# A graph layer on one core: tables on 96 partitions, weights split stepwise, loads between portions of the clear, and a reordered second stage

## The chip, the core and the metric

The kernel runs on one NeuronCore of a Trainium2 chip. The core has five engines with queues of their own: TensorE (PE, with its weight loads PEld), VectorE (DVE), ScalarE (ACT), GpSimd (POOL) and SyncE (SP), which here only issues DMAs. They meet through semaphores. The metric is device time in microseconds (us), the median of several runs.

## The reference

50,000 nodes with 256 features and 50,000 edges, sorted by `dst`. In the call the layer's `idx_i` is `src` and its `idx_j` is `dst`. Everything is float32.

```python
def ssp(x): return jax.nn.softplus(x) - LOG2
h = x @ W_in2f
Wij = (ssp(rbf @ Wf1 + bf1) @ Wf2 + bf2) * dist_cut     # rbf: edge_attr_64
x_ij = h[idx_j] * Wij
m = jax.ops.segment_sum(x_ij, idx_i, num_segments=n_atoms)
m = ssp(m @ Wo1 + bo1) @ Wo2 + bo2
return _layernorm(x + (x + m))
```

## The kernel before

**Groups.** Edges are worked on in G = 98 groups of 512 (the last has 336), as R = 4 rows r of 128. Since the edge sum and the product with Wo1 can change places, the first stage computes for each group: gather `x[dst]` (`xg`, a ring of 8), transpose it, h = x W_in; in parallel the filter from `attr`; the message; its product with Wo1; a product with `same` that adds up edges of equal `src` within the group; and a scatter with addition into the DRAM tensor `acc`. `acc` must first be filled with bo1 - log 2 (the "clear"). The second stage goes over the nodes in 98 groups: fetch `acc`, transpose, softplus, product with Wo2 plus bo2, residual 2x + m, normalisation, store.

**Precision.** Each product is three: every operand is split into a high part (`_h`, type float32r) and a low part (`_l`). ScalarE makes the high parts, VectorE the low ones.

**Order.** Each engine has its order written out: `run((stage, lag), ...)` issues in step s, for each entry, the stage for group s - lag. There is no scheduler.

**Start (before).** VectorE zeroes three tables (L649 to L651); SP then loads dst, bo1, src and the edge weights as tables of 97 rows of 2 KB plus one short row, then all weights and biases (L255 to L261), then issues the clear: 195 DMAs of 256 KB and two more (L265, L267). TensorE turns the tables (L377); VectorE copies `dst_t`, after which GpSimd may gather; VectorE splits all the weights (L683 to L697), and its last operation releases `const_made`, for which TensorE and ScalarE wait ahead of step 0.

**First stage.** GpSimd issues gathers for AHEAD = 21 groups, each waiting until TensorE has turned the x eight groups back (`xt_ps`); only then the scatter of group 0, which also waits for the whole clear; then scatters and the remaining gathers alternate. `sums` is a ring of 11 between `keep_y` and the scatter. ScalarE issues the loads of `attr` and `src` (L525, L530) within its step, just ahead of `keep_y(0)` (L607). The second stage's first eight `xg` loads (L280) wait for the last x transposes.

**Second stage.** The lines of a step s are, by engine:

```python
pe:   run((turn2(0), 0), (out2(0), 2), (turn2(1), 0), (out2(1), 2))
act:  run((expo2, 0), (ssp2_high, 1), (loga2, 0), (deviation, 3))
dve:  run((cap_2, 0), (ssp2_low, 1), (softplus_2, 0), (residual, 2))
pool: run((norm, 0))
```

`turn2` (L494) transposes one half of the features; `out2(q)` (L506, L509) computes two rows r: for each a product of `ones_r` with `bo2_hl`, both on 2 partitions (high and low part of bo2), and six products on 128. `expo2` is L621, `cap_2` (L784, clamp at 2^57 and add 0.5) comes between it and the logarithm `loga2` (L626), `softplus_2` (L790) takes the maximum with the input, `ssp2_high` is L631, `ssp2_low` L674, `residual` L808 (with sums) and L813 (negative mean), `deviation` four squares with sums (L640). On GpSimd `norm` computes the variance plus eps (L357), its power -1/2 (L359) and the four normalised rows (L363). `res` has three buffers (DEPTH), `normed` four; the residual of group g waits for the normalisation of group g - 3.

Of the kernel before, what the change touches and what calls it, by code (L numbers as in the profile page):

```python
# [50 lines left out]
AHEAD = 21  # L51
LOG2 = 0.6931471805599453
EXP_MAX = 2.0 ** 57
# [24 lines left out]
def build(nc, t, out):  # L78
# [7 lines left out]
    TAIL = E - (G - 1) * ROWS  # L86

# [3 lines left out]
    def run(*stages, start=0):  # L91

        for s in range(start, G + max(lag for _, lag in stages)):
            for stage, lag in stages:
                if 0 <= s - lag < G:
                    stage(group(s - lag))
# [3 lines left out]
    with ExitStack() as ctx:  # L103
# [12 lines left out]
        ones = sb("ones", [2, P])  # L116
        ones_r = sb("ones_r", [2, P], F32R)
# [18 lines left out]
        dst_t = sb("dst_t", [P, R, G], I32)  # L136
        spare_i = sb("spare_i", [P, 1], I32)
# [35 lines left out]
        squares = attr[:, 0:2].rearrange("p u r k a -> p (u r k a)").rearrange("p (r d) -> p r d", r=R)  # L173
# [16 lines left out]
        const_made = sem("const_made")  # L190
# [51 lines left out]
        def _(sp):  # L242

            def load_rows(dest, ap, done):
                sp.dma_start(dest[0:G - 1, :], ap[0:(G - 1) * ROWS].rearrange("(g e) -> g e", e=ROWS)).then_inc(done, 16)
                sp.dma_start(dest[G - 1:G, 0:TAIL], ap[(G - 1) * ROWS:E].rearrange("(g e) -> g e", e=TAIL)).then_inc(done, 16)

            sp.wait_ge(rows_zero, 1)
            load_rows(dst_i, t["dst"], dst_in)
            sp.dma_start(bo1[:], t["L0_gnn_bo1"].partition_broadcast(P)).then_inc(bo1_in, 16)  # L250
            load_rows(src_i, t["src"], rows_in)
            load_rows(wgt_f, t["edge_weight1"].rearrange("e a -> (e a)"), rows_in)

            for k in range(2):
                sp.dma_start(wf1[k * A:(k + 1) * A, :], t["L0_gnn_Wf1"]).then_inc(const_in, 16)  # L255
            for w, name in ((w_in, "L0_gnn_W_in2f"), (wf2, "L0_gnn_Wf2"), (wo1, "L0_gnn_Wo1"), (wo2, "L0_gnn_Wo2")):
                sp.dma_start(w[:], t[name].rearrange("(h p) n -> p h n", p=P)).then_inc(const_in, 16)
            for b, name in ((bf1, "L0_gnn_bf1"), (bf2, "L0_gnn_bf2")):
                for h in range(H):
                    sp.dma_start(b[:, h:h + 1], t[name][h * P:(h + 1) * P].rearrange("(p a) -> p a", a=1)).then_inc(const_in, 16)  # L260
            sp.dma_start(bo2[:], t["L0_gnn_bo2"].partition_broadcast(2)).then_inc(const_in, 16)  # L261

            sp.wait_ge(fill_made, 1)
            for c in range(CLEARS):
                sp.dma_start(acc[c * CLEAR * P:(c + 1) * CLEAR * P, :].rearrange("(p k) d -> p (k d)", k=CLEAR), fill[:, 0:CLEAR].rearrange("p k d -> p (k d)")).then_inc(cleared, 16)  # L265
            for a, b in ((CLEARS * CLEAR * P, N), (N, N + R * P)):
                sp.dma_start(acc[a:b, :].rearrange("(p k) d -> p (k d)", k=4), fill[0:(b - a) // 4].rearrange("p k d -> p (k d)")).then_inc(cleared, 16)  # L267

# [18 lines left out]
            for n in range(XRING):  # L287
                fetch_x(group(n))
# [13 lines left out]
        def _(pool):  # L302
# [4 lines left out]
            pool.memset(ones[:], 1.0).then_inc(made, 1)  # L307
            pool.iota(spare_i[:], [[0, 1]], base=N, channel_multiplier=1).then_inc(made, 1)
# [62 lines left out]
        def _(pe):  # L371

            pe.wait_ge(made, 6)
            for k, (rows, arrived, count, done) in enumerate(((dst_f, dst_cast, 1, dst_ps), (src_f, rows_cast, 1, tab_ps), (wgt_f, rows_in, 16 * 4, tab_ps))):
                pe.wait_ge(arrived, count)
                for r in range(R):
                    last = pe.transpose(bank[k][:, r * G:(r + 1) * G], rows[0:G, r::R], ident[0:G, 0:G])  # L377
                last.then_inc(done, 1)

            pe.wait_ge(two_made, 1)  # L380
            for m in range(H):
                for k in range(H):
# [452 lines left out]
```

## Time and profile before

| | us |
|---|---|
| median of 3 runs | 2085.95 |
| lowest, highest | 2079.63, 2088.7 |
| profiled execution | 2090.3 |
| its span, first to last instruction | 2088.5 |
| busy TensorE / VectorE / ScalarE / GpSimd | 1886.3 / 1637.4 / 1550.2 / 1535.3 |
| mean granted clock of TensorE, 1 is full speed | 0.98 |

Busy time alone tells little here: a matmul's end is modelled, so TensorE at 90% is not TensorE at its peak, and on GpSimd the issuing of gathers and scatters counts as work. In the timeline a row is: start, duration, engine, line, operation, output <- inputs, and in brackets how long the engine was idle before it and what ended that. Rows with "x4" are several instructions in one.

### The profile page before, as it was taken

The page shows a single profiled execution, that of the slowest core. Times are in us where ns is not written, and L with a number is a line of the kernel's source. Part 1 is how long each engine was busy: PE and PEld are TensorE (multiplying, and loading weights), DVE is VectorE, ACT ScalarE, POOL GpSimd, SP SyncE. Part 2 cuts the span into 40 slices and gives each one's busy share as a digit, 9 for nine tenths or more (in the row PEclk, how much of TensorE's full clock was granted, in tenths as well). Part 3 has the DMA queues.
Part 4 walks back from the last instruction along what each step waited for, and adds up shares of the span by engine and source line. Part 5 has one row for each costly group of instructions (what it writes and reads, how often), then busy time and mean ns, then how long its engine had stood idle before and what let it go on. Part 6 is the DMA issues. An engine that isn't in the chain of part 4 may idle for free. (4 is left out here: it accounts for less than half of the span.)

```text
span 2088.5 us, 37484 instructions
## 1 busy us (share of the span) xinstructions
PE 1886.3 (90%) x11780; PEld 1606.7 (77%) x11780; DVE 1637.4 (78%) x3663; ACT 1550.2 (74%) x3137; POOL 1535.3 (74%) x1384
## 2 busy tenths in 40 slices
PE   1899999999999999999999898895999999999997
PEld 1788888888888888888887787784777777777775
DVE  2788888888888888888888877783677777777774
ACT  0777888778787787887787776672777777777775
POOL 5422788888888888888888888763677777777776
PEclk9999999999999999999999999996999999999997
DMA  6999566666666666666666666664577777777762
GB/s 204 388 396 388 106 113 120 118 118 112 112 118 119 118 116 109 117 119 117 119 112 112 120 110 119 105 151 98 192 255 254 248 251 253 252 248 253 255 241 104
DMA packets 265299, 363.33 MB, mean 174 GB/s; under 512 B 125848, under 2 KB 177261, under 8 KB 265104
## 3 DMA queue, kind: packets, MB, share of 16 engines
q0 software_dynamic: 75136, 102.45, 29.6%
q1 hardware_dynamic: 72724, 207.27, 28.1%
q10 hardware_dynamic: 117244, 51.22, 10.5%
q8 instruction: 97, 1.59, 0.3%
q14 instruction: 98, 0.80, 0.1%
HBM read 206.71 MB, written 154.12 MB: 173 GB/s over the span
## 5 line engine op out<-in xcount | busy, mean ns | idle before, releaser
L333 POOL DMA_INDIRECT acc<-sums,src_ix x392 | 652.0, 1663 | 142.0 <-issue 111.3
L320 POOL DMA_INDIRECT xg<-in_x,dst_t x392 | 414.7, 1058 | 226.9 <-PE pair L403 106.8
L363 POOL TENSOR_SCALAR sums<-sums,neg_mean,rstd 128x256 f32<-128x256 f32 x392 | 349.1, 904 | 10.2
L478 PE MATMUL pair<-m_h,same 128*128 128x256 f32 (+1 forms) x980 | 253.6, 295 | 50.9 <-ACT sums L607 50.9
L719 DVE SCALAR_TENSOR_TENSOR same<-srcb,src_t,later 128x512 fp32r<-128x512 int32 (+3 forms) x392 | 289.9, 800 | 0.0
L509 PE MATMUL pair<-wo_h,ssp_h 128*128 128x256 f32 (+1 forms) x784 | 264.8, 338 | 0.0
L755 DVE SCALAR_TENSOR_TENSOR m_l<-pair,wgt_t,m_h 128x256 fp32r<-128x256 f32 x392 | 171.7, 480 | 107.2 <-ACT m_h L600 107.2
L478 PEld LDWEIGHTS pair<-m_h,same 128*128 128x128 f32 (+1 forms) x980 | 183.9, 188 | 89.0 <-issue 86.6
L478 PE MATMUL pair<-m_l,same 128*128 128x256 f32 (+1 forms) x980 | 238.3, 279 | 0.0
L392 PE MATMUL pair<-wo_h,msg_h 128*128 128x256 f32 (+1 forms) x784 | 229.8, 293 | 3.3 <-DVE m_l L755 2.8
L509 PE MATMUL pair<-wo_h,ssp_l 128*128 128x256 f32 (+1 forms) x784 | 224.5, 286 | 0.0
L509 PE MATMUL pair<-wo_l,ssp_h 128*128 128x256 f32 (+1 forms) x784 | 224.0, 286 | 0.0
L392 PE MATMUL pair<-wo_h,msg_l 128*128 128x256 f32 (+1 forms) x784 | 221.2, 282 | 0.0
L392 PE MATMUL pair<-wo_l,msg_h 128*128 128x256 f32 (+1 forms) x784 | 221.0, 282 | 0.0
L640 ACT ACTIVATE attr<-sums,neg_mean 128x256 f32<-128x256 f32 x392 | 193.4, 496 | 9.8 <-DVE neg_mean L813 9.8
L674 DVE TENSOR_TENSOR ssp_l<-ssp,ssp_h 128x512 fp32r<-128x512 f32 (+1 forms) x245 | 187.5, 798 | 14.1 <-ACT ssp_h L631 12.3
L600 ACT ACTIVATE m_h<-pair,wgt_t 128x256 fp32r<-128x256 f32 x392 | 164.7, 472 | 44.7 <-PE pair L392 34.6
L506 PE MATMUL pair<-bo_hl,ones_r 2*128 2x256 f32 x392 | 150.6, 384 | 47.1 <-DVE ssp_l L674 47.1
L557 ACT ACTIVATE zs<-pair,bf 128x512 f32<-128x512 f32 x196 | 124.2, 686 | 92.3 <-PE pair L423 92.3
L674 DVE TENSOR_TENSOR msg_l<-msg,msg_h 128x512 fp32r<-128x512 f32 x196 | 135.1, 689 | 73.5 <-ACT msg_h L538 73.5
L509 PEld LDWEIGHTS pair<-wo_h,ssp_h 128*128 128x128 f32 (+1 forms) x784 | 149.9, 191 | 51.3 <-issue 2.7
L478 PEld LDWEIGHTS pair<-m_l,same 128*128 128x128 f32 (+1 forms) x980 | 184.3, 188 | 0.1
(105 smaller groups left out, 5375.3 us busy)
## 6 DMA issues: line engine op xcount, KB each, us to landing
acc<-fill SPq DMA_DIRECT2D x195, 256.0 KB
xg<-in_x SPq DMA_DIRECT2D x97, 512.0 KB, 4.3
sums<-acc SPq DMA_DIRECT2D x97, 512.0 KB, 4.2
out<-sums SPq DMA_DIRECT2D x97, 512.0 KB, 2.9
attr<-in_edge_attr ACTq DMA_DIRECT2D x194, 128.0 KB, 4.6
srcb<-in_src ACTq DMA_DIRECT2D x97, 256.0 KB, 4.3
xg<-in_x,dst_t POOLq DMA_INDIRECT x392, 3.7
acc<-sums,src_ix POOLq DMA_INDIRECT x392
```

The source lines that it names most:

```text
L320: pool.indirect_dma_start(xg[0:g.p, g.xs, r], None, t["x"], bass.IndirectOffsetOnAxis(ap=dst_t[0:g.p, r, g.n:g.n + 1], axis=0)).then_inc(x ...
L333: pool.indirect_dma_start(acc, bass.IndirectOffsetOnAxis(ap=src_ix[g.slot][0:g.p, r:r + 1], axis=0), sums[0:g.p, g.slot, r], None, compute ...
L363: last = pool.tensor_scalar(normed[0:g.p, g.n % NRING, r], res[0:g.p, u, r], neg_mean[0:g.p, u, r:r + 1], rstd[0:g.p, u, r:r + 1], ALU.add ...
L392: last = pe.matmul(o, a, b, start=n == 0, stop=n == len(terms) - 1)
L478: last = pe.matmul(o, same[0:g.p, g.par, FROM[a] + b - a, 0:g.p], m[0:g.p, a], start=a == 0 and m is m_h, stop=a == b and m is m_l)
L506: pe.matmul(o, ones_r[:, 0:g.p], bo2_hl[:], start=True, stop=False)
L509: last = pe.matmul(o, sp2[:, g.par, h, r, 0:g.p], w[:, h, :], start=False, stop=h == H - 1 and sp2 is ssp2_l)
L600: act.activation(m_h[0:g.p, r], bank[6][0:g.p, k * D:(k + 1) * D], ACT.Copy, scale=col(wgt_t, r, g)).then_inc(mh_sb, 1)
L640: last = act.activation(squares[0:g.p, r], res[0:g.p, u, r], ACT.Square, bias=neg_mean[0:g.p, u, r:r + 1], accum_out=square[0:g.p, u, r:r ...
L674: dve.tensor_tensor(out_, whole, high.bitcast(F32), ALU.subtract).then_inc(done, count)
L719: dve.scalar_tensor_tensor(out=same[0:g.p, g.par, FROM[a]:FROM[a] + R - a, 0:g.p], in0=sources[:, a:R], scalar=col(src_t, a, g), in1=later ...
L755: dve.scalar_tensor_tensor(out=m_l[0:g.p, r], in0=bank[6][0:g.p, k * D:(k + 1) * D], scalar=col(wgt_t, r, g), in1=m_h[0:g.p, r].bitcast(F3 ...
```

## The change

- *Tables.* `MAIN` = 96 of the 98 rows are loaded as one table; the last two groups go into small tiles of their own (`dst_last`, `src_last`, `wgt_last`), laid out as needed without a transpose. Only these are zeroed.
- *Weights.* All weight and bias loads move from SP to ScalarE's queue. `const_made` is gone: TensorE waits for each weight where it first uses it (`wf1_made`, `w_in_made`, ...). ScalarE makes the high parts ahead of its step 1, VectorE the rest ahead of its steps 1, 2 and 3. `run` got the argument `before` for it.
- *Loads and clear.* `load_attr` and `load_src` move from ScalarE to SP and stand between portions of the clear: 24 DMAs first, then 15 a step. The load of `attr` n waits for the transposes of group n - 3 (`at_ps`), that of `src` n - 1 for the comparison of group n - 4 (`same_ready`). AHEAD is 20.
- *Second stage.* Both transposes come ahead of both `out2`. `bo2_hl` and `ones_r` take 128 partitions, rows 2 to 127 of bo2 being zero. The clamp and the addition leave `cap_2`: the logarithm gets the bias 0.5, and the maximum first takes min(ln, 40). One of the four squares moves from ScalarE to VectorE (`deviation_last`), for which `norm` waits too. The first loads of x are issued in the order in which their buffers come free.

```diff
-AHEAD = 21
+AHEAD = 20
+FIRST_CLEARS = 24
+CLEARS_A_STEP = 15
-EXP_MAX = 2.0 ** 57
+LN_MAX = 40.0
+    MAIN = G - G % 16
...
+            sp.dma_start(dst_i[0:MAIN, :], t["dst"][0:MAIN * ROWS].rearrange("(g e) -> g e", e=ROWS)).then_inc(dst_in, 16)
+            sp.wait_ge(last_zero, 3)
...
+            clear_to(FIRST_CLEARS)
...
+            for n in range(2, G + 1):
+                if n < G:
+                    load_attr(n)
+                load_src(n - 1)
+                clear_to(FIRST_CLEARS + (n - 1) * CLEARS_A_STEP)
...
-            for n in range(XRING):
-                fetch_x(group(n))
+            for n in range(G - XRING, G):
+                fetch_x(group(n % XRING))
...
                 pool.wait_ge(square_sb, g.n + 1)
+                pool.wait_ge(square_dve, g.n + 1)
...
-            pe.wait_ge(const_made, 1)
             run((w_of(1), 2), (turn_a, 0), (summed(0), 3), (h_of(0), 1), (summed(1), 3), (filter1, 0), (turn_x(0), 0),
-                (out1(0), 2), (turn_x(1), 0), (w_of(0), 1), (h_of(1), 1), (out1(1), 2))
+                (out1(0), 2), (turn_x(1), 0), (w_of(0), 1), (h_of(1), 1), (out1(1), 2), before={1: filter_bias})
...
-            run((turn2(0), 0), (out2(0), 2), (turn2(1), 0), (out2(1), 2))
+            run((turn2(0), 0), (turn2(1), 0), (out2(0), 2), (out2(1), 2))
...
-            act.wait_ge(const_made, 1)
-            run((next_attr, 0), (keep_y(0), 4), ... (msg_high(0), 2), (load_src, 0))
+            run((keep_y(0), 4), ... (msg_high(0), 2), before={1: weights})
...
-                act.wait_ge(cap2, g.n + 1)
+                act.wait_ge(exp2, g.n + 1)
                 z = grown[g.par][:].rearrange("m h n -> m (h n)")
-                act.activation(z, z, ACT.Ln).then_inc(ln2, 1)
+                act.activation(z, z, ACT.Ln, bias=half[:]).then_inc(ln2, 1)
...
-                for r in range(R):
+                for r in range(R - 1):
...
+                (ssp_low(1), 1), (compare, 2), before={1: first_weights, 2: tables, 3: second_weights})
...
+                dve.scalar_tensor_tensor(out=squares[0:g.p, R], in0=res[0:g.p, u, r], scalar=neg_mean[0:g.p, u, r:r + 1], in1=res[0:g.p, u, r],
+                                         op0=ALU.add, op1=ALU.mult, accum_out=square[0:g.p, u, r:r + 1]).then_inc(square_dve, 1)
...
-            run((cap_2, 0), (ssp2_low, 1), (softplus_2, 0), (residual, 2))
+            run((ssp2_low, 1), (deviation_last, 3), (softplus_2, 0), (residual, 2))
```

Where the change moves instructions, the engines' rows read as follows (output <- inputs, shape, and in brackets the semaphores that an instruction waits for).

TensorE in a step of the second stage, before: transposes of one half (L494), a block of out2 with its bias product (L506), and the second half's transposes behind it.

```order
L494 MATMUL pair1<-ident,sums 128x128 [waits ssp2_sb,m_got3]
L494 MATMUL pair1<-ident,sums 128x128 x3
L506 MATMUL pair3<-bo2_hl,ones_r 128x256 [waits res_sb,ssp2l_sb]
L509 MATMUL pair3<-wo2_h,ssp_h 128x256
L509 MATMUL pair3<-wo2_l,ssp_h 128x256
L509 MATMUL pair3<-wo2_h,ssp_l 128x256
```

After:

```order
L537 MATMUL pair1<-ident,sums 128x128 [waits ssp2_sb,m_got3]
L537 MATMUL pair1<-ident,sums 128x128 x3
L537 MATMUL pair1<-ident,sums 128x128 [waits ssp2_sb,m_got3]
L537 MATMUL pair1<-ident,sums 128x128 x3
L551 MATMUL pair3<-bo2_hl,ones_r 128x256 [waits res_sb,ssp2l_sb]
L554 MATMUL pair3<-wo2_h,ssp_h 128x256
```

The second half's transposes moved ahead of the wait for `ssp2l_sb`.

VectorE in a step of the second stage, before:

```order
L784 TENSOR_SCALAR h_sb<-h_sb 128x1024 [waits exp2]
L674 TENSOR_TENSOR ssp_l<-ssp,ssp_h 128x1024 [waits o_ps,ssp2h_sb]
L790 TENSOR_TENSOR msg<-pair1,h_sb 128x1024 [waits ssp2l_sb,ln2]
L808 SCALAR_TENSOR_TENSOR sums,total<-xg,pair3 128x256 [waits o_ps,norm_sb,x_got3]
L808 SCALAR_TENSOR_TENSOR sums,total<-xg,pair3 128x256
```

After:

```order
L699 TENSOR_TENSOR ssp_l<-ssp,ssp_h 128x1024 [waits o_ps,ssp2h_sb]
L877 SCALAR_TENSOR_TENSOR attr,square<-sums,neg_mean 128x256 [waits square_dve,veps_sb,mean_sb]
L846 SCALAR_TENSOR_TENSOR msg<-h_sb,pair1 128x1024 [waits ssp2l_sb,ln2]
L864 SCALAR_TENSOR_TENSOR sums,total<-xg,pair3 128x256 [waits o_ps,norm_sb,x_got3]
L864 SCALAR_TENSOR_TENSOR sums,total<-xg,pair3 128x256
```

The clamp in front is gone, and a square of group s - 3 stands behind the low part.

SP at the start of the clear, before:

```order
L261 DMA bo2<-in_L0_gnn_bo2 2x256
L265 DMA acc<-fill 128x512 [waits fill_made]
L265 DMA acc<-fill 128x512 x194
L267 DMA acc<-fill 20x1024
L267 DMA acc<-fill 128x1024
```

After:

```order
L287 DMA acc<-fill 128x512 x15
L259 DMA attr<-in_edge_attr_64 128x4x64 [waits at_ps]
L259 DMA attr<-in_edge_attr_64 128x4x64
L264 DMA srcb<-in_src 128x512 [waits same_ready]
L287 DMA acc<-fill 128x512 x15
```

Two waits on the loop's progress now stand ahead of each later portion of the clear.

## Rows read from the trace of the kernel before

**Rows 1.** Timeline of one step of the second stage, columns as above.
```profile
1704.70 1.03 ACT L621 ACTIVATE h_sb<-pair 128x1024 f32<-128x1024 f32 x1 [1.41 <-PE pair L494]
1704.77 3.62 POOL L363 TENSOR_SCALAR sums<-sums,neg_mean,rstd 128x256 f32<-128x256 f32 x4
1705.76 0.69 DVE L784 TENSOR_SCALAR h_sb<-h_sb 128x1024 f32<-128x1024 f32 x1 [1.40 <-ACT h_sb L621]
1706.71 1.25 DVE L674 TENSOR_TENSOR ssp_l<-ssp,ssp_h 128x1024 fp32r<-128x1024 f32 x1 [0.25 <-ACT ssp_h L631]
...
1708.01 0.38 PE L506 MATMUL pair<-bo_hl,ones_r 2*128 2x256 f32 x1 [0.47 <-DVE ssp_l L674]
...
1708.55 0.28 PE L509 MATMUL pair<-wo_l,ssp_h 128*128 128x256 f32 x1
1708.66 0.28 PE L509 MATMUL pair<-wo_h,ssp_l 128*128 128x256 f32 x1
...
1709.23 0.38 PE L506 MATMUL pair<-bo_hl,ones_r 2*128 2x256 f32 x1
...
1709.68 0.19 POOL L357 TENSOR_SCALAR veps<-square 128x4 f32<-128x4 f32 x1 [1.29 <-ACT attr L640]
...
1711.00 1.03 ACT L621 ACTIVATE zs<-pair 128x1024 f32<-128x1024 f32 x1 [1.41 <-PE pair L494]
```

**Rows 2.** Timeline of GpSimd (POOL), first stage and the second stage's first operation.
```profile
197.85 0.95 POOL L320 DMA_INDIRECT xg<-in_x,dst_t  x1 [8.96 <-PE pair L403]
...
211.39 0.95 POOL L320 DMA_INDIRECT xg<-in_x,dst_t  x1 [8.84 <-PE pair L403]
...
216.40 1.64 POOL L333 DMA_INDIRECT acc<-sums,src_ix  x1 [0.30 <-issue]
...
1436.47 1.49 POOL L333 DMA_INDIRECT acc<-sums,src_ix  x1 [0.30 <-issue]
...
1470.66 0.19 POOL L357 TENSOR_SCALAR veps<-square 128x4 f32<-128x4 f32 x1 [32.70 <-ACT attr L640]
```

**Rows 3.** GpSimd's groups, 500 to 800 us: count | busy, mean ns | idle before.
```profile
L333 POOL DMA_INDIRECT acc<-sums,src_ix x97 | 160.5, 1655 | 30.6 <-issue 27.2 <-DMA acc<-sums,src_ix 1.8 <-ACT sums L607 1.5
L320 POOL DMA_INDIRECT xg<-in_x,dst_t x78 | 86.4, 1108 | 23.8 <-issue 20.1 <-PE pair L403 3.7
```

**Rows 4.** Timeline of the start.
```profile
14.04 0.43 DVE L655 CAST sums<-sums 128x512 f32<-128x512 int32 x1 [11.50 <-DMA sums<-in_dst]
...
16.42 1.22 POOL L320 DMA_INDIRECT xg<-in_x,dst_t  x1 [14.06 <-DVE dst_t L659]
...
52.35 1.91 PE L403 MATMUL pair<-ident,xg 128*128 128x128 f32 x8
```

**Rows 5.** The page's DMA issues: count, median us from issue to landing.
```profile
xg<-in_x,dst_t POOLq DMA_INDIRECT x392, 3.7
```

**Rows 6.** Timeline of SP's queue during the clear.
```profile
59.64 139.33 SPq L265 DMA_DIRECT2D acc<-fill  x167
```

**Rows 7.** Groups by form, 1600 to 1900 us: count | busy us, mean ns | idle before.
```profile
L640 ACT ACTIVATE attr<-sums,neg_mean 128x256 f32<-128x256 f32 x192 | 94.7, 496 | 0.0
...
L808 DVE SCALAR_TENSOR_TENSOR sums<-xg,pair 128x256 f32<-128x256 f32 x192 | 68.6, 409 | 0.0
```

**Rows 8.** Windows: busy PE, PEld, DVE, ACT, POOL; granted clock, DMA share, GB/s.
```profile
1600.00:1650.00 50.00, 46.23 (x288) 36.75 (x287) 36.67 (x96) 38.75 (x89) 38.22 (x48) 1.00 0.73 251
```

**Rows 9.** Timeline of the end of the second stage.
```profile
2060.16 0.38 PE L506 MATMUL pair<-bo_hl,ones_r 2*128 2x256 f32 x1 [1.00 <-DVE ssp_l L674]
...
2061.46 0.58 PE L506 MATMUL pair<-bo_hl,ones_r 2*128 2x256 f32 x1
...
2062.71 1.23 DVE L674 TENSOR_TENSOR ssp_l<-msg,ssp_h 128x1024 fp32r<-128x1024 f32 x1
...
2063.15 2.84 POOL L363 TENSOR_SCALAR sums<-sums,neg_mean,rstd 128x256 f32<-128x256 f32 x4
...
2067.46 2.18 POOL L363 TENSOR_SCALAR sums<-sums,neg_mean,rstd 128x256 f32<-128x256 f32 x4
```

More of the change, by code:

```diff
@@ L86, in build, with run @@
     TAIL = E - (G - 1) * ROWS
+    MAIN = G - G % 16
+    assert 0 < G - MAIN <= 2
     def group(n):
         return Group(n, n % 2, n // 2 + 1, ROWS if n < G - 1 else TAIL)
-    def run(*stages, start=0):
-        for s in range(start, G + max(lag for _, lag in stages)):
+    def run(*stages, before={}):
+        for s in range(G + max(lag for _, lag in stages)):
+            if s in before:
+                before[s]()
             for stage, lag in stages:
@@ L252, in _ @@
[L252 to L260, printed above, removed]
@@ L261, in _, with load_attr @@
-            sp.dma_start(bo2[:], t["L0_gnn_bo2"].partition_broadcast(2)).then_inc(const_in, 16)
-            sp.wait_ge(fill_made, 1)
-            for c in range(CLEARS):
-                sp.dma_start(acc[c * CLEAR * P:(c + 1) * CLEAR * P, :].rearrange("(p k) d -> p (k d)", k=CLEAR), fill[:, 0:CLEAR].rearrange("p k d -> p (k d)")).then_inc(cleared, 16)
+            def load_attr(n):
+                g, u = group(n), n % ARING
+                wait(sp, at_ps, n - ARING + 1)
+                for k in range(2):
+                    sp.dma_start(attr[0:g.p, u, :, k, :], rows_of(t["edge_attr_64"], g).rearrange("(p r) a -> p r a", r=R)).then_inc(attr_in[u], 16)
@@ new lines, in load_src @@
+            def load_src(n):
+                g, u = group(n), n % SRING
+                wait(sp, same_ready, (n - SRING + 1) * R)
+                sp.dma_start(srcb[:, u, 0:g.rows], rows_of(t["src"], g).partition_broadcast(P)).then_inc(srcb_in[u], 16)
+            flat = t["edge_weight1"].rearrange("e a -> (e a)")
+            sp.dma_start(dst_i[0:MAIN, :], t["dst"][0:MAIN * ROWS].rearrange("(g e) -> g e", e=ROWS)).then_inc(dst_in, 16)
+            sp.wait_ge(last_zero, 3)
+            for k, p, rows in last_of(t["dst"]):
+                sp.dma_start(dst_last[0:p, k], rows).then_inc(dst_last_in, 16)
@@ L608, in keep_y @@
                 return stage
-            for n in range(ARING - 1):
-                load_attr(group(n))
-            act.wait_ge(const_made, 1)
-            run((next_attr, 0), (keep_y(0), 4), (msg_high(1), 3), (ssp_high(0), 2), (ssp_high(1), 2), (keep_h(0), 2), (absolute(0), 1),
+            run((keep_y(0), 4), (msg_high(1), 3), (ssp_high(0), 2), (ssp_high(1), 2), (keep_h(0), 2), (absolute(0), 1),
                 (absolute(1), 1), (expo(0), 1), (m_high(0), 3), (keep_y(1), 4), (expo(1), 1), (x_high(0), 1), (loga(0), 1),
-                (loga(1), 1), (x_high(1), 1), (keep_h(1), 2), (m_high(1), 3), (a_high, 0), (msg_high(0), 2), (load_src, 0))
+                (loga(1), 1), (x_high(1), 1), (keep_h(1), 2), (m_high(1), 3), (a_high, 0), (msg_high(0), 2), before={1: weights})
             def expo2(g):
```

238 lines of the change are left out of this document (143 added, 95 removed).

## Prediction

> **What bounds the kernel now.** I read the page's 40 slices first: they divide the span at about 1440 us into a first stage (gather, products, scatter) and a second one (output layer, residual, normalisation). Then I read each boundary in the timeline.
>
> *Second stage.* It is a loop of 97 equal steps. ScalarE starts its exponential at 1704.70 and again at 1711.00 [rows 1]: one step is 6.3 us (6.29 in the mean). In it ScalarE sits idle 1.41 us, VectorE 1.40 + 0.25, GpSimd 1.29, TensorE 0.47 (each idle figure is the bracket of a row). When every engine waits, none is the bound: a ring of waits is. It reads: transposes done -> exponential at 1704.70 -> `ssp_high` -> `ssp_low` at 1706.71 (it waited for ScalarE) -> the bias product at 1708.01 (it waited for `ssp_low`) -> out2(0), two blocks of r at 1.22 us each (1708.01 to 1709.23) -> the transposes turn2(1), queued behind out2(0) on TensorE -> the next exponential, which waited for them. That ring is the 6.29 us.
>
> *First stage.* GpSimd issues the gathers and scatters. From 216.40, when the first scatter goes out, to 1436.47, the last one, it hardly rests: 392 scatters at (160.5 + 30.6) / 97 = 1.97 us and the 308 gathers left at (86.4 + 23.8) / 78 = 1.41 us make 1207 of the 1220 us [rows 2, 3]. So the stage's end is set by when scattering starts. That in turn is held by the gather at 211.39, which waited 8.84 us for TensorE's transposes of an earlier group; with AHEAD at 21 all of group 20's gathers stand before the first scatter. TensorE itself began its x transposes only at 52.35 [rows 4].
>
> **The change part by part.**
>
> *Start.* The table dst was in and being cast at 14.04, after an 11.50 us wait; the first gather went out at 16.42; the loop then waited until 52.35 for the queue of loads and the splitting of all weights [rows 4]. Now dst is the first DMA, of 96 rows, with nothing zeroed ahead of it; the weights go on ScalarE's queue, and only wf1 is needed in step 0. No row shows a 96-row table load. Its ends are the usual landing of a small gather, 3.7 us [rows 5], and the old 11.50; I take 4 to 5, near the first, since the packets of ordinary tiles land so. Then cast, the load of bo1 and fill (both queued ahead on VectorE), transposes and copy: first gather near 9.5. Four gathers (about 1.25 each) and 3.7 to land give group 0 at 18 to 19. The weight work is not gone. It lies in the first steps: four copies on ScalarE, about seven small operations in `first_weights`, thirteen in `tables`, six in `second_weights` on VectorE, some 2 to 3 us beyond the cover of a filling pipeline. So TensorE's steps run about 31 us earlier (bounds 20 and 37).
>
> *Scatter start.* AHEAD = 20 asks for one group less, so what releases the last pre-gather is the wait that ended at 197.85, not 211.39 [rows 2]: 197.85 - 31 = 167, and four gathers make it 172. The other condition is the clear, now cut in portions of 15. One clear costs SP 139.33 / 167 = 0.834 us [rows 6], 15 of them 12.5, less than a step's 13.5 (197.85 to 211.39). But SP's portion n waits for a comparison of group n - 4; the last portion (6 clears) is released near 167, and 6 x 0.834 = 5 plus 3.7 to land gives 176. The clear sets it: first scatter at 176 (bounds 168 and 188) against 216.40. Queued behind SP's waits are the attr and src loads; each is issued about a step before its use, so I cost them at nothing. Their cover is that step; if SP ran a portion late TensorE would wait about 5 us in each of the first twelve steps, which is why the upper bound is 188.
>
> *Rest of the first stage.* GpSimd has four more gathers to do afterwards, 4 x 1.41 = 5.6. The loads leaving ScalarE's queue take away a small wait of TensorE for `keep_y`; with GpSimd as bound that is worth nothing. So the last scatter goes out at 176 + 1220.1 + 5.6 = 1401.7, against 1436.47: **-34.8 us**. The clamp, the order of fetch_x (still behind the last src load, so still a burst) and the 96-partition tables change nothing further there.
>
> *Bias product over 128 rows.* A block of r takes 1.22 us (1708.01 to 1709.23) for one 2-row and six 128-row products. Two full products in a row start 0.11 to 0.12 apart (1708.55, 1708.66) [rows 1]. Seven at 0.117 are 0.82: 0.40 less per block, 1.6 per step. The bound on the other side is nothing gained, if the delay belongs to the first product of a block rather than to its two rows. I take the full gain: of the seven products only this one has two rows, and the one behind it is late too. TensorE's own step is then 6.29 - 0.47 - 1.6 = 4.2.
>
> The Trainium skill has two rules on this. "TensorE: Matmul & The Clock Gate", section Why this matters for your kernels, says that one product of small K takes as long as a full one; by it the bias edit saves nothing and a step would stay near 5.8. "TensorEngine Tiling (Array Packing)", Key Properties, says that a change of tiling mode drains the engine; by it the step is the 4.2. The trace's 1.22 speaks for the second.
>
> *Transposes first.* Both transposes of group g now stand ahead of out2(g - 2). The ring then runs over two steps: transposes, exponential 1.03, high part 1.05, low part 1.25, out2 4 x 0.82, about 7.5 us for two steps, 3.8 each. It no longer binds. What is late next?
>
> *ScalarE:* 6.29 - 1.41 = 4.88, less one square of 0.50 [rows 7] = 4.4 (the new bias operand of Ln perhaps 0.05). *VectorE:* 6.29 - 1.65 = 4.64, less the clamp 0.69, plus the fourth square, nearest a residual piece of 0.41 [rows 7] = 4.4; the clamp inside the maximum I cost at 0 to 0.1. *DMA:* its share is 0.73 of a step [rows 8], so 4.6 at most. *GpSimd:* 6.29 - 1.29 = 5.00, of which the four normalisations are 3.62. These stretch beside VectorE: with VectorE almost at rest they take 2.18 (2067.46) [rows 9]. In the loop 1.44 us are added beside 0.69 + 1.25 = 1.94 us of clamp and `ssp_low`, 0.74 per us; at 2063.15 0.66 are added beside 0.79 us of `ssp_low` alone, 0.84 per us. Afterwards the clamp is gone and the square, which reads two SBUF tiles, is there: 1.25 + 0.41 = 1.66 us x 0.74 to 0.84 = 1.23 to 1.39. GpSimd's step: 5.00 - 3.62 + 2.18 + 1.31 = **4.87 us**. As res has three buffers, VectorE's residual waits for the normalisation three groups back, and its low part then falls wholly beside the next one, so nothing of the overlap is escaped. GpSimd binds.
>
> The "GPSIMD Engine Reference" of the Trainium skill, Key points, names the cause: GpSimd shares its SBUF interfaces with VectorE, contended by operations in a 2-port mode or with two SBUF inputs. By it the moved square does slow GpSimd; without it the step would be about 4.55.
>
> *Sum of the second stage.* From the last scatter to group 0's normalisation were 1470.66 - 1436.47 = 34.2 us [rows 2]; without clamp and with transposes ahead I take 28 (bounds 22 and 34). Then 97 x 4.87 = 472.4. The old tail was 2088.5 - 1470.66 - 97 x 6.29 = 7.7, shortened by fast last steps; I take 10. In all 510.4 against 652.0: **-141.6**.
>
> Span 1401.7 + 510.4 = 1912.1, plus the 1.8 us around it (2090.3 - 2088.5) = 1914. That is 176.4 below the profiled 2090.3, which stands 4.35 above the median 2085.95; so 2085.95 - 176.4 = 1909.6, **1910**.
>
> **The rivals.** (a) *The bias product gains nothing.* TensorE's step stays 6.29 - 0.47 = 5.8 and binds in place of GpSimd: 97 x 0.93 = 90 more, 2000. For it: the first rule above. Against: the 0.11 spacing of full products. (b) *GpSimd is not slowed by the moved square,* or escapes part of `ssp_low`; then ScalarE and VectorE bind at 4.4 to 4.5: 97 x -0.42, 1869. (c) *The start gains little:* loads, gathers and portions of the clear share SP and the DMA queues, and first scatters move by only 10 us or so: 1935 to 1945. (d) *Slower than before.* TensorE idles 4.87 - 4.2 = 0.67 us in each step, and its granted clock could fall. At 2060.16 a wait of 1.00 came ahead of a fall: the same product took 0.38 and from 2061.46 0.58 [rows 9]. At 1.2 GHz TensorE's 4.2 become about 8.1, and the step is 8.1 instead of 4.87. The gain of 176 is used up when 176 / (97 x 3.23) = 56% of the steps run so; all of them give 2220. Against: with a wait of 0.47 in every step the granted clock is 1.00 [rows 8]. That the change does not do what it says is possible in the first stage alone, where SP's waits order the clear; it is (c).
>
> **How the numbers follow.** Forecast 0.63; (a) 0.08; (b) 0.12; (c) 0.10; (d) 0.07, of which 0.04 ends above the old time. The forecast's own spread is 1885 to 1935: GpSimd's step 4.79 to 4.95, -8 and +8, scatter start -8 and +12, fill -6 and +6. Adding (b) and (c) gives 1865 to 1970, which leaves out (a) and (d). A difference under 0.5% is about what a measurement of this kernel cannot tell from none. Faster 0.95, within 0.5% 0.01, slower 0.04.
>
> **What would show it.** First gather near 9.5, TensorE's first x transposes near 19, first scatter near 176, last one near 1402; in the second stage steps of 4.87 us in which GpSimd has no idle time before its first operation and VectorE's residual waits for it; bias products 0.28 long at 0.12 spacing; the granted clock 1.00. Wrong if TensorE shows blocks over 1 us, if GpSimd waits for ScalarE, or if the scatters start after 190.

## The result and the profile after

| | before | after |
|---|---|---|
| median, us | 2087.32 (4 runs, 2079.63 to 2092.38) | 1909.26 (4 runs, 1907.56 to 1909.53) |
| span of the profiled execution, us | 2088.5 | 1907.3 |
| last scatter issued at, us | 1436.47 | 1447.43 |
| from there to the end, us | 652.0 | 459.9 |

The ratio is 0.915, 95% interval 0.912 to 0.918. The forecast was 1910 us, and by its total it could not have been closer. That closeness is luck, as the last two rows tell: the first stage was to end 34.8 us earlier and ends 11.0 us later, and the second stage was to gain 141.6 us and gains 192.1. Two errors of 46 and 50 us cancel.

The page of after, for the whole span (busy us, share, instructions; then DMA traffic in 40 slices):

```profile
PE 1752.6 (92%) x11780; PEld 1593.9 (84%) x11780; DVE 1599.3 (84%) x3760; ACT 1493.7 (78%) x2945; POOL 1452.6 (76%) x1385
...
GB/s 348 379 361 366 156 118 108 120 117 110 119 114 113 119 110 106 113 111 112 110 105 121 113 106 111 109 112 114 98 153 118 334 359 360 364 363 361 359 363 187
```

**Start.** The timeline of after, VectorE, GpSimd and TensorE, against [rows 4]:

```profile
3.52 0.42 DVE L703 CAST sums<-sums 96x512 f32<-96x512 int32 x1 [2.53 <-DMA sums<-in_dst]
...
6.98 1.22 POOL L351 DMA_INDIRECT xg<-in_x,dst_t  x1 [4.37 <-DVE dst_t L709]
...
10.77 1.16 PE L409 MATMUL pair<-ident,sums 96*128 96x96 f32 x6
...
17.59 1.97 PE L437 MATMUL pair<-ident,xg 128*128 128x128 f32 x8 [1.25 <-DMA xg<-in_x,dst_t]
```

The table of dst is being cast at 3.52 instead of 14.04, the first gather goes out at 6.98 instead of 16.42 (forecast 9.5), and the x transposes begin at 17.59 instead of 52.35. SP's queue in the same stretch:

```profile
9.38 16.00 SPq L287 DMA_DIRECT2D acc<-fill  x24
25.42 1.24 SPq L292 DMA_DIRECT2D acc<-fill  x2
26.70 2.98 SPq L259 DMA_DIRECT2D attr<-in_edge_attr  x2
29.72 4.88 SPq L264 DMA_DIRECT2D srcb<-in_src  x1
34.64 8.11 SPq L287 DMA_DIRECT2D acc<-fill  x15
```

The third group's attributes (line 259) leave only at 26.70, behind 24 clears. TensorE waits for such loads 12.9 us in all between 20 and 200 us. At the other end of the clear GpSimd waits:

```profile
178.88 0.94 POOL L351 DMA_INDIRECT xg<-in_x,dst_t  x1 [0.30 <-issue]
198.88 1.74 POOL L364 DMA_INDIRECT acc<-sums,src_ix  x1 [19.06 <-DMA acc<-fill]
```

The last early gather was out at 178.88; the first scatter then waited 19.06 us for the clear and went at 198.88 (forecast 176; before 216.40).

**First stage.** GpSimd's groups of after, 500 to 800 us, answer to [rows 3]:

```profile
L364 POOL DMA_INDIRECT acc<-sums,src_ix x94 | 160.8, 1711 | 42.6 <-issue 37.7 <-DMA acc<-sums,src_ix 4.9
L351 POOL DMA_INDIRECT xg<-in_x,dst_t x76 | 74.5, 980 | 23.2 <-issue 23.2
```

94 scatters instead of 97 fit in. The gathers are shorter (980 against 1108 ns), the scatters longer (1711 against 1655), and the idle time ahead of scatters has grown from 30.6 to 42.6 us. From the first to the last scatter it is 1248.6 us, not 1220.1.

**Second stage.** One step of after, rows of ScalarE, VectorE and GpSimd, against [rows 1] (columns: start, us, engine, line):

```profile
1598.45 2.90 POOL L395 TENSOR_SCALAR sums<-sums,neg_mean,rstd 128x256 f32<-128x256 f32 x4
...
1600.12 1.11 ACT L667 ACTIVATE h_sb<-pair 128x1024 f32<-128x1024 f32 x1
...
1600.53 0.41 DVE L864 SCALAR_TENSOR_TENSOR sums<-xg,pair 128x256 f32<-128x256 f32 x1
...
1601.03 1.16 ACT L677 ACTIVATE ssp_h<-ssp 128x1024 fp32r<-128x1024 f32 x1
...
1601.98 1.25 ACT L672 ACTIVATE h_sb<-h_sb,half 128x1024 f32<-128x1024 f32 x1
...
1602.21 1.23 DVE L699 TENSOR_TENSOR ssp_l<-ssp,ssp_h 128x1024 fp32r<-128x1024 f32 x1
...
1602.82 2.90 POOL L395 TENSOR_SCALAR sums<-sums,neg_mean,rstd 128x256 f32<-128x256 f32 x4
1603.01 0.60 ACT L686 ACTIVATE attr<-sums,neg_mean 128x256 f32<-128x256 f32 x1
...
1603.36 0.49 DVE L877 SCALAR_TENSOR_TENSOR attr<-sums,neg_mean 128x256 f32<-128x256 f32 x1
...
1604.49 1.11 ACT L667 ACTIVATE zs<-pair 128x1024 f32<-128x1024 f32 x1
```

The step is 1604.49 - 1600.12 = 4.37 us, and 97 of them make 424. No row of ScalarE, GpSimd or TensorE has a bracket: three engines run without idle time, and the timeline alone doesn't say which of them the others follow. VectorE's residual (line 864) starts at 1600.53 without waiting, in the middle of a normalisation (1598.45 to 1601.35). The windows show the same (busy PE, PEld, DVE, ACT, POOL; clock, DMA share, GB/s), against [rows 8]:

```profile
1600.00:1650.00 50.00, 50.00 (x414) 48.36 (x414) 49.22 (x151) 50.00 (x103) 46.84 (x71) 1.00 0.99 361
```

### The profile page after: what moved, and what is told of

It is laid out like the page before. It is cut to its first block and busy times, and to the rows that moved or that the text cites. A ratio compares the mean times of both kernels' runs of the same rounds, so it can differ in the third digit from the quotient of the medians.

```text
span 1907.3 us, 37602 instructions
## 1 busy us (share of the span) xinstructions
PE 1752.6 (92%) x11780; PEld 1593.9 (84%) x11780; DVE 1599.3 (84%) x3760; ACT 1493.7 (78%) x2945; POOL 1452.6 (76%) x1385
## 5 line engine op out<-in xcount | busy, mean ns | idle before, releaser
L364 POOL DMA_INDIRECT acc<-sums,src_ix x392 | 664.6, 1695 | 202.7 <-issue 144.4
L351 POOL DMA_INDIRECT xg<-in_x,dst_t x392 | 385.1, 982 | 193.9 <-issue 116.4
L395 POOL TENSOR_SCALAR sums<-sums,neg_mean,rstd 128x256 f32<-128x256 f32 x392 | 283.1, 736 | 10.2
L426 PE MATMUL pair<-wo_h,msg_h 128*128 128x256 f32 (+1 forms) x784 | 235.8, 301 | 3.8 <-DVE m_l L817 3.8
L426 PE MATMUL pair<-wo_h,msg_l 128*128 128x256 f32 (+1 forms) x784 | 227.1, 290 | 0.0
L554 PE MATMUL pair<-wo_h,ssp_h 128*128 128x256 f32 (+1 forms) x784 | 221.2, 282 | 0.0
L437 PE MATMUL pair<-ident,xg 128*128 128x128 f32 (+1 forms) x784 | 126.5, 288 | 90.4 <-DMA xg<-in_x,dst_t 90.4
L437 PEld LDWEIGHTS pair<-ident,xg 128*128 128x128 f32 (+1 forms) x784 | 99.3, 149 | 107.8 <-DMA xg<-in_x,dst_t 96.1
L426 PE MATMUL pair<-ssp_h,wf_h 128*128 128x512 f32 x392 | 163.9, 418 | 0.0
L686 ACT ACTIVATE attr<-sums,neg_mean 128x256 f32<-128x256 f32 x294 | 161.3, 661 | 3.1 <-DVE neg_mean L869 3.1
```

Of the source, the lines that this page charges most:

```text
L351: pool.indirect_dma_start(xg[0:g.p, g.xs, r], None, t["x"], bass.IndirectOffsetOnAxis(ap=dst_t[0:g.p, r, g.n:g.n + 1], axis=0)).then_inc(x ...
L364: pool.indirect_dma_start(acc, bass.IndirectOffsetOnAxis(ap=src_ix[g.slot][0:g.p, r:r + 1], axis=0), sums[0:g.p, g.slot, r], None, compute ...
L395: last = pool.tensor_scalar(normed[0:g.p, g.n % NRING, r], res[0:g.p, u, r], neg_mean[0:g.p, u, r:r + 1], rstd[0:g.p, u, r:r + 1], ALU.add ...
L426: last = pe.matmul(o, a, b, start=n == 0, stop=n == len(terms) - 1)
L437: last = pe.transpose(bank[q][:, c:c + g.p], xg[0:g.p, g.xs, 2 * q + k, h * P:(h + 1) * P], ident[0:g.p, 0:g.p])
L554: last = pe.matmul(o, sp2[:, g.par, h, r, 0:g.p], w[:, h, :], start=False, stop=h == H - 1 and sp2 is ssp2_l)
```

## Experiments

Steps are start to start of GpSimd's first operation near 1700 us, where every kernel is in its second stage. Times of one set are compared with `before` on the same chip; it took 2088.7, 2078.6 and 2107.9 us in the three sets. In set 1 its runs spread from 2072.6 to 2102.2 us, so the readings below rest on the steps and scatter times of the traces rather than on the totals.

| kernel | set | us | first scatter | last scatter | step, us |
|---|---|---|---|---|---|
| `before` | | 2087.3 | 216.4 | 1436.5 | 6.29 |
| `after` | | 1909.3 | 198.9 | 1447.4 | 4.37 |
| `old_full_bias` | 1 | 2026.5 | 216.6 | 1440.9 | 5.71 |
| `old_turn_first` | 1 | 2028.2 | 218.5 | 1434.7 | 5.75 |
| `s2_two_rows` | 1 | 2038.9 | 198.2 | 1448.8 | 5.73 |
| `s1_loads_act` | 1 | 1866.9 | 190.3 | 1401.9 | 4.37 |
| `s1_sp_late` | 2 | 1882.1 | 196.6 | 1417.7 | 4.37 |
| `old_both` | 2 | 1930.0 | 217.9 | 1433.2 | 4.78 |
| `s2_square_act` | 2 | 1957.0 | 197.7 | 1451.0 | 4.86 |
| `s2_no_bias` | 2 | 1910.3 | 199.0 | 1447.6 | 4.37 |
| `s2_three_parts` | 3 | 1893.9 | 206.4 | 1447.5 | 4.25 |
| `s2_early_clamp` | 3 | 1996.8 | 205.9 | 1447.8 | 5.29 |
| `s1_no_attr` | 3 | 1890.5 | 206.2 | 1427.0 | 4.37 |

### Where the second stage's gain comes from

**The bias product alone, in the kernel before** (`old_full_bias`).

```diff
-        ones_r = sb("ones_r", [2, P], F32R)
+        ones_r = sb("ones_r", [P, P], F32R)
-        bo2_hl = sb("bo2_hl", [2, D], F32R)
+        bo2_hl = sb("bo2_hl", [P, D], F32R)
```

> The kernel before with the bias product made full-row (128 rows instead of 2) and nothing else changed. Stage 2 took 6.29 us a step there, in a ring: the second half's transposes stand behind the first half's products. Ring theory: two of the four blocks of r stand in the ring, each 0.40 us shorter, so the step falls by 0.8 to 5.5 us and the time by 97 x 0.8 = 78 us, to about 2009 us. Rival 1, TensorE's own work bound the step: all four blocks count, 1.6 us less, 4.7 us a step, -155 us, about 1932 us. Rival 2, the row count of a product makes no difference to the ones around it: no change, 2087 us.

Step 5.71: the ring theory, with its size off, 0.58 us instead of 0.8. TensorE in `old_full_bias`, the two blocks in the ring and the transposes behind them:

```profile
1606.45 0.38 PE L509 MATMUL pair<-bo_hl,ones_r 128*128 128x256 f32 x1 [1.23 <-DVE ssp_l L677]
...
1606.67 0.28 PE L512 MATMUL pair<-wo_h,ssp_h 128*128 128x256 f32 x1
...
1607.38 0.28 PE L509 MATMUL pair<-bo_hl,ones_r 128*128 128x256 f32 x1
...
1608.22 0.60 PE L497 MATMUL pair<-ident,sums 128*128 128x128 f32 x4
```

and, for `before`, the transposes behind the second block of [rows 1]:

```profile
1710.36 0.60 PE L494 MATMUL pair<-ident,sums 128*128 128x128 f32 x4
```

The first block takes 0.93 us instead of 1.22: its bias product ends a wait, and the successor still starts 0.22 later. The second, up to the transposes, takes 0.84 instead of 1.13 (1709.23 to 1710.36), since it has no 2-row product behind it that comes late. Each saves 0.29 instead of 0.40, and that is the 0.58.

**The order alone, in the kernel before** (`old_turn_first`).

```diff
-            run((turn2(0), 0), (out2(0), 2), (turn2(1), 0), (out2(1), 2))
+            run((turn2(0), 0), (turn2(1), 0), (out2(0), 2), (out2(1), 2))
```

> The kernel before with both halves' transposes of the second stage ahead of the products, nothing else changed: the bias product stays at 2 rows. TensorE's own work is 8 transposes at 0.94 us and four blocks of 1.22 us, 5.8 us together. If the order removes the ring, the step falls from 6.29 to 5.8 us, -47 us, about 2040 us. Rival, the ring was never what bound: no change, 2087 us. Rival, the ring goes and TensorE's blocks overlap the transposes' loads: 5.5 us, 2010 us.

Step 5.75, TensorE without idle time: the ring is gone and TensorE's own 5.8 binds at once. So each edit alone is worth 0.5 to 0.6 us.

**Both** (`old_both`: the two diffs above together).

> The kernel before with both TensorE edits of the second stage: full-row bias product and both halves' transposes first. Each alone gave a step of about 5.7 us against 6.29. The clamp and the fourth square stay where they were. TensorE's own work is 4.4 us; ScalarE has four squares, 4.9 us; VectorE 4.4. Expected: step 4.9 us, ScalarE without idle time, about 2088 - 97 x 1.4 = 1950 us. Rival, TensorE binds or GpSimd, stretched by four two-input operations of VectorE: 4.4 or 5.1 us, 1905 or 1972 us. Rival, the two edits overlap and the second adds nothing: 5.7 us, 2027 us.

Step 4.78 instead of 6.29: together 1.51 us, more than the 0.58 + 0.54 of the two alone, since each removes the bound that hides the other. ScalarE has no idle time (busy 50.00 of 50 us), and its starts lie 0.91 (exp), 0.95 (high part), 0.94 (Ln) and 4 x 0.49 (squares) apart, 4.77 in sum.

**Two rows again, in the kernel after** (`s2_two_rows`).

```diff
-                        pe.matmul(o, ones_r[:, 0:g.p], bo2_hl[:], start=True, stop=False)
+                        pe.matmul(o, ones_r[0:2, 0:g.p], bo2_hl[0:2], start=True, stop=False)
```

> The kernel after with the bias product over 2 rows again, all else as after. Theory: each block of r returns from 0.83 to 1.22 us, TensorE binds alone at 0.94 + 4 x 1.22 = 5.8 us a step instead of 4.37: +97 x 1.45 = +140 us, about 2050 us, all of it in stage 2. Rival, the gain of stage 2 came from the order and the late clamp: the step stays near 4.4 to 4.6, 1910 to 1930 us.

Step 5.73. One block of r on TensorE, from one bias product to the next:

```profile
1606.54 0.38 PE L551 MATMUL pair<-bo_hl,ones_r 2*128 2x256 f32 x1
1606.85 0.38 PE L554 MATMUL pair<-wo_h,ssp_h 128*128 128x256 f32 x1
1607.07 0.28 PE L554 MATMUL pair<-wo_l,ssp_h 128*128 128x256 f32 x1
...
1607.54 0.28 PE L554 MATMUL pair<-wo_h,ssp_l 128*128 128x256 f32 x1
1607.75 0.38 PE L551 MATMUL pair<-bo_hl,ones_r 2*128 2x256 f32 x1
```

A block is 1.21 us (1607.75 - 1606.54); with 128 rows it is 0.83. Three starts are late: the 2-row product itself comes 0.21 after the one ahead of it (1607.54 to 1607.75), its successor 0.31 later and the next one 0.22, against 0.12 between full products. The excess, 0.09 + 0.19 + 0.10 = 0.38 us, is the whole difference of a block.

### What sets the 4.37 us

**Fourth square back on ScalarE** (`s2_square_act`).

```diff
-                for r in range(R - 1):
+                for r in range(R):
                     last = act.activation(squares[0:g.p, r], res[0:g.p, u, r], ACT.Square,
-            run((ssp2_low, 1), (deviation_last, 3), (softplus_2, 0), (residual, 2))
+            run((ssp2_low, 1), (softplus_2, 0), (residual, 2))
```

> The kernel after with the fourth square back on ScalarE. ScalarE was without idle time at 4.37 us a step; if its operations keep their length it binds at 4.37 + 0.49 = 4.86 us, +47 us, about 1956 us. Rival, ScalarE's operations were only stretched to fill the step by the others that work beside them: step 4.4 to 4.6 us, 1912 to 1930 us. Rival, GpSimd was the bound and is relieved of the moved square: 4.1 us or less, 1880 us.

Step 4.86, ScalarE busy 50.00 of 50, as if ScalarE alone decided. GpSimd waits 0.33 for it in each step now.

**No bias product** (`s2_no_bias`: the line of `s2_two_rows` taken out, so bo2 is missing in the output).

> The kernel after with the bias product of the second stage left out (bo2 is not added to the output), so that TensorE has 4 of its 36 operations less, 0.47 us a step. If TensorE is what sets the 4.37 us, the step falls until the next engine binds, below 4.2 us: at least 15 us less, 1890 us or less. If ScalarE or GpSimd sets it, TensorE gets 0.4 us of idle time and the step stays at 4.37 us, 1909 us.

The step stays at 4.37 with 4 of TensorE's 36 operations gone:

```profile
1600.00:1650.00 50.00, 45.70 (x371) 43.07 (x370) 49.20 (x153) 50.00 (x103) 46.85 (x70) 1.00 0.98 359
```

TensorE, though busy in every moment in `after`, does not set the step.

**One square less on ScalarE** (`s2_three_parts`).

```diff
-                for r in range(R - 1):
+                for r in range(1, R - 1):
```

> The kernel after with one of ScalarE's three squares of a step left out (the variance's first part is a constant, so those rows are normalised wrongly). ScalarE has 4.37 - 0.49 = 3.88 us of work a step. If ScalarE alone set the 4.37 us, the step falls to the next bound: VectorE's 4.30 us or TensorE's 8 x 0.1175 + 28 x 0.1185 = 4.26 us, so 4.26 to 4.30 us, 7 to 11 us less, near 1900 us. If GpSimd, which had no idle time either, binds beside it, the step stays at 4.37 us, 1909 us.

Step 4.25. ScalarE now waits 0.24 us, and TensorE and VectorE fill the step:

```profile
1600.00:1650.00 50.00, 50.00 (x425) 49.65 (x425) 49.59 (x156) 47.00 (x82) 46.84 (x72) 1.00 1.00 368
```

So ScalarE's 4.37 was the bound, with the next one 0.12 us behind it. That one is most likely TensorE's own 4.26, but VectorE and GpSimd are as full there, and no run separates them. GpSimd had no idle time at steps of 5.29, 4.78, 4.37 and 4.25 us alike: its four normalisations took 3.82, 3.21, 2.90 and 2.77 us there. Since it keeps up with 4.25, it wasn't what held the step at 4.37: its length adapts to the pace, at least down to 4.25. The DMA engines are at a share of 0.99 in `after` and 1.00 here, yet no engine waits for a transfer between 1500 and 1850 us in either; the loads of x take 6.8 us to land in `after` (4.3 before) and come early enough.

**Clamp early again** (`s2_early_clamp`).

```diff
-                act.wait_ge(exp2, g.n + 1)
+                act.wait_ge(cap2, g.n + 1)
-                act.activation(z, z, ACT.Ln, bias=half[:]).then_inc(ln2, 1)
+                act.activation(z, z, ACT.Ln).then_inc(ln2, 1)
-            run((ssp2_low, 1), (deviation_last, 3), (softplus_2, 0), (residual, 2))
+            run((cap_2, 0), (ssp2_low, 1), (deviation_last, 3), (softplus_2, 0), (residual, 2))
```

> The kernel after with the clamp of the second stage early again: VectorE takes the minimum and adds one half in an operation of its own (0.69 us) between exp and Ln, and Ln has no bias tile. ScalarE's Ln falls from 1.04 to 0.95 us, its work to 4.28 us; VectorE's work rises from 4.30 to 4.99 us and binds: +0.62 us a step, +60 us, about 1969 us. Rival, the longer path from exp through the clamp to Ln is hidden and VectorE's operations were stretched only because they had the time: step near 4.4 us, 1912 us.

Step 5.29, more than either theory said. VectorE is busy 49.7 of 50 us and waits for nobody, while ScalarE waits 0.9 us for it in each step. Its own operations have stretched: the clamp takes 0.91 us instead of 0.69 [rows 1], the square 0.70 instead of 0.49 in `after`.

These are rows of VectorE, and ScalarE's wait:

```profile
1700.32 0.70 DVE L885 SCALAR_TENSOR_TENSOR attr<-sums,neg_mean 128x256 f32<-128x256 f32 x1
...
1703.66 0.91 DVE L848 TENSOR_SCALAR h_sb<-h_sb 128x1024 f32<-128x1024 f32 x1
...
1704.60 1.06 ACT L674 ACTIVATE h_sb<-h_sb 128x1024 f32<-128x1024 f32 x1 [0.91 <-DVE h_sb L848]
```

Both ran beside normalisations; but in [rows 1] the clamp did so too and took 0.69, so what stretched it here is not settled. GpSimd has no idle time here either, so it isn't excluded that the two hold each other up. Given the moved square, the late clamp is worth 0.92 us a step, about 89 us: without it VectorE's chain, not ScalarE, would have set the step. The worth of such edits isn't additive: in `old_both`, with all four squares on ScalarE, the early clamp (0.69 us there) binds nothing. Four steps show it together: 4.78 with neither edit (`old_both`), 4.86 with the late clamp alone (`s2_square_act`), 5.29 with the moved square alone (`s2_early_clamp`), 4.37 with both. Either edit alone makes the step longer.

### Where the first stage's gain went

**Loads back on ScalarE's queue** (`s1_loads_act`: load_attr and load_src as in the kernel before, all clears in one row on SP).

```diff
-            clear_to(FIRST_CLEARS)
+            clear_to(CLEARS)
-            for n in range(2, G + 1):
-                if n < G:
-                    load_attr(n)
-                load_src(n - 1)
-                clear_to(FIRST_CLEARS + (n - 1) * CLEARS_A_STEP)
-            run((keep_y(0), 4), (msg_high(1), 3), ...
+            run((next_attr, 0), (keep_y(0), 4), (msg_high(1), 3), ...
```

> The kernel after with the loads of edge_attr and src back on ScalarE's queue and all clears issued in one row on SyncE, as before. In the kernel after the clear moved 353 to 360 GB/s with the loads in its own queue, against 395 before. Theory 1, the shared queue is what stretches the clear: first scatter near 183 us instead of 198.9. Theory 2, on top of it the loads in SyncE's queue also delay the landing of the scatters, for which GpSimd waits about 0.45 us a group in the kernel after and not in the one before: the period of a group falls from 12.8 to 12.5 us, last scatter near 1400 instead of 1447, time about 1860. If only theory 1 holds: last scatter 1432 to 1447, time 1893 to 1909. Rival 3, TensorE's 13.07 us a step is the bound of stage 1: the last scatter does not move, 1909 us.

1866.9 us, ratio to `before` 0.895 (interval 0.889 to 0.901), shorter than `before` and `after`. First scatter 8.6 us earlier than in `after`, last one 45.5. Windows of `after` and of `s1_loads_act` during the clear (the last number is GB/s):

```profile
60.00:180.00 120.00, 114.88 (x724) 101.52 (x723) 102.47 (x215) 93.85 (x182) 37.58 (x40) 0.99 1.03 364
```

```profile
60.00:180.00 120.00, 115.31 (x733) 100.69 (x733) 104.26 (x220) 94.28 (x183) 33.96 (x37) 1.00 1.07 397
```

The rest, 37 us, comes after the first scatter. GpSimd's groups of `s1_loads_act`, 500 to 800 us:

```profile
L345 POOL DMA_INDIRECT acc<-sums,src_ix x96 | 158.2, 1648 | 31.0 <-issue 28.0 <-DMA acc<-sums,src_ix 2.7 <-DVE src_ix L790 0.3
L332 POOL DMA_INDIRECT xg<-in_x,dst_t x80 | 86.6, 1083 | 24.4 <-issue 20.4 <-PE pair L418 4.0
```

These are the numbers of [rows 3] again. Idle times over 0.3 us ahead of scatters sum to 1.9 us there and to 14.0 us (15 times) in `after`. Queue or moment?

**Same queue, later** (`s1_sp_late`).

```diff
                 wait(sp, at_ps, n - ARING + 1)
+                if n >= 16:
+                    sp.wait_ge(ah_sb, n - 2)
...
                 wait(sp, same_ready, (n - SRING + 1) * R)
+                if n >= 16:
+                    sp.wait_ge(ah_sb, n + 1)
```

> The kernel after with the loads still in SyncE's queue, but from group 16 on each load also waits until ScalarE has reached the place in its own order at which it issued that load in the kernel before (a step later than the slot comes free). The first scatter stays near 199 us. If the moment at which the loads run (not the queue) is what delays the scatters' landing, the groups from 300 us on take 12.5 us as with the loads in ScalarE's queue, last scatter near 1410, time about 1872. If it is the queue, the period stays at 12.9 and 12.65 us, last scatter near 1447, 1909 us.

The waits fall from 14.0 to 0.1 us, first to last scatter takes 1221.1 us instead of 1248.6, time 1882.1. So it is the moment. It accounts for the whole loss up to group 90: from the first scatter to that group's first one `after` takes 1151.0 us, and `s1_sp_late` 1121.0, `s1_loads_act` 1120.9 and `before` 1120.7. The 9.5 us by which `s1_loads_act` (1211.6 in all) still leads `s1_sp_late` arise in the last seven groups, and why is open. Timeline of `after`, GpSimd and SP:

```profile
605.98 1.56 POOL L364 DMA_INDIRECT acc<-sums,src_ix  x1 [0.30 <-issue]
607.16 0.33 SPq L264 DMA_DIRECT2D srcb<-in_src  x1
607.53 1.27 SPq L259 DMA_DIRECT2D attr<-in_edge_attr  x2
```

and of `s1_sp_late`:

```profile
607.16 1.55 POOL L368 DMA_INDIRECT acc<-sums,src_ix  x1 [0.31 <-issue]
...
611.38 0.33 SPq L268 DMA_DIRECT2D srcb<-in_src  x1
```

In `after` the loads, waiting for nothing but a free buffer, start 1.2 us after the group's fourth scatter was issued, while its rows are under way. The next group's first scatter waits for three things, its indices, its sums and the landing of all earlier scatters (`added`). In the 15 groups of `after` that waited between 500 and 800 us the first two had been ready for 124 us or more, so it is the landing. In `s1_sp_late` the loads start 4.2 us after the fourth scatter. TensorE's granted clock is not the cause: between 800 and 1100 us it was 0.94 in the mean in `after` (1.00 in `before`), and 0.94 in `s1_sp_late` too.

**No attribute loads** (`s1_no_attr`: load_attr returns for groups from 16 on, so these groups use old attributes).

```diff
             def load_attr(n):
+                if n >= LOADED:
+                    return
```

> The kernel after with the loads of edge_attr left out from group 16 on (those groups work on the attributes of earlier ones). What is left in SyncE's queue after the clear is one load of src a group. First scatter unchanged near 199 us. If it is the transfers of edge_attr, issued about 1.2 us after the fourth scatter, that delay the landing of the scatters, the waits ahead of the first scatter of a group (14 us in 300) go and the period falls from 12.9 to 12.5 us or less: last scatter 1410 or earlier, 1872 us or less. If the waits have another cause (TensorE's pace, the src load), the last scatter stays near 1447, 1909 us.

First to last scatter takes 1220.8 us. The two kernels of its set whose first stage is that of `after` take 1241.1 (`s2_three_parts`) and 1241.9. The waits of 500 to 800 us fall from 2.9 to 0.1. The loads of `src` are still there, so it is those of the attributes that cost the 20 us. That set's clear was slower (351 GB/s, first scatter at 206), and the waits in these 300 us were 2.9 and not 14.0 us, and yet 20 us were lost over the stage. That the loss depends on how loads and scatters fall together would fit this, but is not shown.

## The prediction, step by step

- **Start: right, and a little better.** Steps begin 34.8 us earlier (forecast 31 or a little more). The first gather goes out 2.5 us sooner than forecast. The loads that the forecast priced at nothing cost 12.9 us of TensorE's time; it did not matter, since GpSimd waited for the clear.
- **First scatter at 176: wrong, 198.9.** By the forecast's own sign ("if the scatters start after 190") this part failed. The failed step is "each is issued about a step before its use, so I cost them at nothing". It priced a clear by SP's issue rate in [rows 6], where no load shared the queue. In `after` SP's portions begin 13.86 us apart (65.92 and 79.78), 11.5 for 15 clears and 2.4 for the loads behind them, with nothing waited for in between, where the forecast had 12.5 in all. So SP's last portion leaves at 190.61 instead of near 167. The traffic is 364 GB/s, against 397 with the loads on ScalarE's queue. It is what rival (c) said, in a smaller size; the sentence that bounded it, "a portion late", gave 188.
- **Rest of the first stage unchanged: wrong by 23 us** (1248.6 against 1220.1 + 5.6). The failed step is "with GpSimd as bound that is worth nothing", said of the loads leaving ScalarE's queue. The forecast looked at what the loads had kept waiting, not at what they would meet. Moving a transfer to a queue that issues as soon as its buffer is free changes its moment, and this moment lay on the landing of the scatters.
- **Bias over 128 rows: right.** Forecast 1.22 to 0.82 per block, measured 1.21 against 0.83. The rule of the Trainium skill that spoke for it, the drain at a change of tiling mode ("TensorEngine Tiling (Array Packing)", Key Properties), agrees with `s2_two_rows`, where the two successors of each 2-row product start 0.31 and 0.22 us later; the rule of equal time for small K ("TensorE: Matmul & The Clock Gate", Why this matters for your kernels) is one of a single product, which no run here times by itself, and it does not hold for the row that the product stands in.
- **Transposes first, ring gone: right** (`old_turn_first` runs at TensorE's own 5.75).
- **TensorE 4.2, ScalarE 4.4, VectorE 4.4: right.** The step is 4.37 with ScalarE as the bound; TensorE and VectorE fit into the 4.25 of `s2_three_parts`. **DMA "4.6 at most": too high, without consequence**; 4.25 was reached at a share of 1.00.
- **GpSimd binds at 4.87: wrong.** The failed step is "nothing of the overlap is escaped". VectorE's residual does not wait for the normalisation that is under way (1600.53 above). Of `ssp_low`'s 1.23 us only 0.62 lie beside the normalisations (1602.82 to 1603.44), and 0.42 of the square: 0.74 us more than the undisturbed 2.16, or 0.7 per us, just below the forecast's own rate of 0.74 to 0.84. It was rival (b), escaping part of `ssp_low`, at 0.12, and its 4.4 to 4.5 was a shade high. The missing half microsecond, 97 times, is 48 of the 50 us.
- **Fill 28, tail 10: right** (26.1 and 9.8).

So rivals (b) and (c), each given about one chance in ten, both came true in essence, the one for -50 us and the other, with an unforeseen stretch behind it, for +46. The range held them because they have opposite signs; that they are nearly equal in size is luck. The clock stayed at 1.00 in the second stage, so (d) did not come.

What stays open: why GpSimd settles where the overlap just fits the step (the rows show that it does, at four step lengths, not how; in no run was its own work changed), what stretched VectorE's own operations in `s2_early_clamp`, and whether loads delay the scatters by their share of the DMA engines or by the memory behind them. In `s1_loads_act` the queue and the row of clears were changed together, so the 33 GB/s are not split between them.

## What to carry to other kernels

When an edit moves a transfer to a queue of its own, ask at which moment it will now run and what else is in flight then, not only who waited for it before; here the loads, free to start with their buffer, ran just behind the last scatter of each group, on whose landing the next group waited. When three engines show no idle time, take a known amount of work from each in turn: only the bound answers in full (here -0.47 us on TensorE gave 0, +0.49 on ScalarE gave +0.49, and -0.49 there gave -0.12, up to the next bound). A forecast made of a stage each is checked stage by stage: a right total can hide two wrong halves.

## What was not expected of the hardware

- A matmul of 2 rows among ones of 128 delays its two successors, by 0.19 and 0.10 us over the usual 0.12 spacing, and comes itself 0.09 late (`s2_two_rows`).
- VectorE's operations can stretch too, not only GpSimd's: in `s2_early_clamp` the clamp took 0.91 us instead of 0.69 and the square 0.70 instead of 0.49, while GpSimd's four normalisations took 3.82 us, against 2.90 in `after` and 2.16 at its undisturbed end.
- ScalarE's durations differ from kernel to kernel at the same pace: exponential, high part and logarithm take 1.11, 1.16 and 1.25 us in `after` and 1.20, 1.24 and 1.32 in `s2_no_bias`, both with a step of 4.37, while their starts lie 0.91, 0.95 and 1.03 or 1.04 apart in both. Its pace is read from starts, not from durations.
